# Causal mask by matmul, clamp split between VectorE and GpSimd, finer turns and a new order in a four-lane Flamingo block

## What is computed

```python
# layer 2, cross attention
attn = jnp.einsum('bhqd,bhkd->bhqk', q, k) * scale
attn = jnp.clip(attn, -CLAMP, CLAMP)            # CLAMP = 10000
attn = jax.nn.softmax(attn, axis=-1)
...
# layer 2, inner transformer ("self")
mask = jnp.triu(jnp.ones((s, s), dtype=bool), 1)
a = jax.nn.softmax(jnp.where(mask, -1000000000.0, a), axis=-1)
...
# layer 0, "bit": act_quant, one scale for each row (token)
scale = 127.0 / jnp.clip(jnp.max(jnp.abs(x), axis=-1, keepdims=True), 1e-05)
return jnp.clip(jnp.round(x * scale), -128, 127) / scale
```

## Time and profile before

| | us |
|---|---|
| median of 3 runs | 2759.86 (2751.84 to 2760.4) |
| the profiled execution, its own time | 2746.58 |
| its span, first to last instruction | 2745.4 |
| PE / PEld busy | 2523.2 / 2047.6 |
| DVE busy | 2182.1 |
| ACT busy | 1674.9 |
| POOL busy | 1134.7 |

### The profile page before, as it was taken

How to read it: one execution, slowest core, us unless ns; L and a number is a source line. 1 busy time by engine, 2 the same in 40 slices (tenths; PEclk the granted TensorE clock), 3 DMA queues, 4 the chain that set the end, 5 groups by cost and what they waited for, 6 DMA issues and landing times.

```text
span 2745.4 us, 66343 instructions
## 1 busy us (share of the span) xinstructions
PE 2523.2 (92%) x26308; PEld 2047.6 (75%) x26308; DVE 2182.1 (79%) x4794; ACT 1674.9 (61%) x4539; POOL 1134.7 (41%) x1981
## 2 busy tenths in 40 slices
PE   6897989898899989899999999999998989999999
PEld 4676767777677767777777777777777878778777
DVE  7778687888788686887777777778878787778998
ACT  4565767666566666666566556556666565556544
POOL 2132323323443543434554544434243333335776
PEclk9898989999899999999999999999999999999999
DMA  6000000000011221000011221000000000000110
GB/s 193 3 21 15 17 9 19 17 13 23 11 48 45 72 68 49 26 13 29 15 53 50 78 82 44 28 25 16 15 26 22 17 17 23 22 5 21 32 39 26
DMA packets 84190, 92.49 MB, mean 34 GB/s; under 512 B 15333, under 2 KB 77289, under 8 KB 83881
## 3 DMA queue, kind: packets, MB, share of 16 engines
q1 hardware_dynamic: 75432, 59.91, 7.1%
q0 software_dynamic: 8448, 28.34, 3.6%
HBM read 65.36 MB, written 22.85 MB: 32 GB/s over the span
## 4 chain that ended last, share of the span: by engine, by line
PE 46%; DVE 35%; ACT 7%; POOL 6%; issue 4%; DMA 1%; SPq 0%; DVEq 0%; POOLq 0%
PE psum L353 11%; PE psum L346 8%; DVE tiny L745 6%; DVE big L753 5%; PE psum L377 5%; PE psum L412 5%; PE psum L386 3%; PE psum L547 2%; PE psum L370 2%; PE psum L427 2%; DVE big L832 2%; PE psum L360 2%; DVE big L836 2%; DVE xn L726 2%; PE psum L367 2%
## 5 line engine op out<-in xcount | busy, mean ns | idle before, releaser
L1240 ACT ACTIVATE big<-big 128x512 f32<-128x512 f32 x512 | 312.3, 629 | 177.6 <-DVE big L753 176.0
L745 DVE TENSOR_REDUCE tiny<-psum 128x8 f32<-128x1024 f32 x256 | 312.3, 1220 | 43.5 <-PE psum L412 38.4
L753 DVE TENSOR_TENSOR big<-psum,tiny 128x512 f32<-128x512 f32 x512 | 329.4, 685 | 8.8
L1401 POOL TENSOR_SCALAR tiny<-mv 128x1 f32<-128x1 f32 x224 | 55.2, 246 | 675.6 <-DVE mv L716 673.7
L412 PE MATMUL psum<-head_keys,small 64*128 64x256 f32 x2048 | 293.9, 407 | 21.1 <-ACT big L1202 6.8
L386 PE MATMUL psum<-ident,big 64*128 64x64 f32 x5120 | 254.9, 233 | 37.9 <-ACT big L1240 18.8
L386 PEld LDWEIGHTS psum<-ident,big 64*128 64x128 f32 x5120 | 211.4, 142 | 103.7 <-ACT big L1240 43.5
L1418 POOL TENSOR_TENSOR head_keys<-big,head_rows 128x512 f32<-128x512 f32 x256 | 266.3, 1049 | 0.4
L1202 ACT ACTIVATE big<-psum 128x512 f32<-128x512 f32 x384 | 212.8, 598 | 63.9 <-PE psum L386 59.6
L1443 POOL TENSOR_TENSOR big<-big,tiny 128x512 f32<-128x512 f32 x128 | 136.7, 1074 | 271.0 <-DVE tiny L788 270.3
L412 PEld LDWEIGHTS psum<-head_keys,small 64*128 64x128 f32 x2048 | 187.3, 192 | 71.0 <-issue 46.0
(11 more groups left out here) (336 smaller groups left out, 6633.3 us busy)
## 6 DMA issues: line engine op xcount, KB each, us to landing
ctxT<-in_ctxT SPq DMA_DIRECT2D x64, 128.0 KB, 2.2
after_L_xattn<-x SPq DMA_DIRECT2D x64, 128.0 KB, 1.7
mixture_out<-spare SPq DMA_DIRECT2D x46, 128.0 KB, 1.7
x_in<-in_x SPq DMA_DIRECT2D x32, 128.0 KB, 2.2
mixture_in<-xn SPq DMA_DIRECT2D x32, 128.0 KB, 1.7
x_in<-after_L_xattn SPq DMA_DIRECT2D x32, 128.0 KB, 2.1
w_bits<-after_L_xattn SPq DMA_DIRECT2D x32, 128.0 KB, 2.3
spare<-in_L_w SPq DMA_DIRECT2D x2, 1024.0 KB, 6.4
```

Of the source, the lines that this page charges most:

```text
L745: dve.tensor_reduce(top, s8, AX.X, ALU.max).then_inc(*t.dve.tell(p, f"{l}.top{r}"))
L753: dve.tensor_tensor(t.e[half], s8[:, mine, :], top[:, mine].rearrange("p (h o) -> p h o", o=1).to_broadcast([P, CH, S]), ALU.subtract).the ...
L1240: last = act.activation(flat, flat, ACT.Exp, scale=DH ** -0.5)
```

## The change

1. **Causal mask.** The DVE pass L742 is gone. Ahead of the scores of `self`, PE writes the mask into the banks with 4 bf16 matmuls of 256 columns (`causal_rows`), and the scores are accumulated on top. The two bf16 constants `sooner` and `masked` are made on POOL during setup.
2. **Clamp.** The DVE pass L738 is gone. The 8 maxima are clamped (128x8), the subtraction becomes a `scalar_tensor_tensor` that also holds the lower bound, and POOL then takes the minimum with 0 on each half (128x512, four times per lane and pass); the exponential waits for POOL.
3. **Row scales.** `diag` and `diag2` are gone; PE transposes the scale column, broadcast over 128 columns.
4. **Finer turns.** On DVE a turn now ends after nearly every instruction whose result the next one needs; on PE long groups of matmuls are split in two or three turns.
5. **Order.** All five strings of `ORDER` are new.

```diff
-def features_T(pe, bank, wt, src, outs):
-    for j, n in enumerate(outs):
+def features_T(pe, bank, wt, src, outs, j0=0):
+    for j, n in enumerate(outs, j0):
...
+def causal_rows(pe, m, t):
+
+    for k in range(2):
+        for half in range(2):
+            rows = slice(half * P // 2, (half + 1) * P // 2)
+            later = t.ab[:, half, :].rearrange("p (h s) -> p h s", s=S)[:, :, k * P // 2:(k + 1) * P // 2]
+            pe.matmul(later, m.sooner[rows, k, :],
+                      m.masked[rows, :].rearrange("p (o s) -> p o s", o=1).to_broadcast([P // 2, CH, P // 2]),
+                      start=k == 0, stop=False)
...
     for r in range(2):
-        pe.wait_ge(*t.pool.at(p, f"{l}.keys{r}"))
         if r == 0:
             pe.wait_ge(*t.act.at(p, f"{l}.v" if l == "self" else f"{l}.q"))
         else:
             pe.wait_ge(*t.act.at(p, f"{l}.eT1"))
+        if l == "self":
+            causal_rows(pe, m, t)
+            yield
+        pe.wait_ge(*t.pool.at(p, f"{l}.keys{r}"))
...
-    context_values(pe, t.b, t.a, t, m.kv[l], range(KD)).then_inc(*t.pe.tell(p, f"{l}.kv"))
+    context_values(pe, t.a, t, m.kv[l], range(KD))
+    yield
+    context_rest(pe, t.b, t.a, t, m.kv[l], range(KD)).then_inc(*t.pe.tell(p, f"{l}.kv"))
...
-    pe.wait_ge(*t.dve.at(p, f"{l}.diag"))
-    pe.matmul(t.b[:, 0:S], m.ones[:], t.diag, start=True, stop=True).then_inc(*t.pe.tell(p, f"{l}.rows"))
+    pe.wait_ge(*t.dve.at(p, f"{l}.sc"))
+    pe.transpose(t.b[:, 0:S], t.tiny[:, 4:5].to_broadcast([P, S]), m.ident[:]).then_inc(*t.pe.tell(p, f"{l}.rows"))
...
-    features_T(pe, t.a, m.w["up"], t.xnT, range(0, 4)).then_inc(*t.pe.tell(p, f"{l}.up0"))
+    features_T(pe, t.a, m.w["up"], t.xnT, range(0, 2))
+    yield
+    features_T(pe, t.a, m.w["up"], t.xnT, range(2, 4), 2).then_inc(*t.pe.tell(p, f"{l}.up0"))
...
     dve.bn_stats(t.stats[:], src).then_inc(*t.dve.tell(p, f"{l}.st{sub}"))
+    yield
     dve.wait_ge(*t.dve.at(p, f"{l}.st{sub}"))
...
         dve.wait_ge(*t.pe.at(p, f"{l}.s{r}"))
+        dve.tensor_reduce(top, s8, AX.X, ALU.max).then_inc(*t.dve.tell(p, f"{l}.top{r}"))
+        yield
+        dve.wait_ge(*t.dve.at(p, f"{l}.top{r}"))
         if l == "L2":
-            flat = t.ab.rearrange("p r s -> p (r s)")
-            dve.tensor_scalar(flat, flat, CLAMP / DH ** -0.5, -CLAMP / DH ** -0.5, ALU.min, ALU.max
+            dve.tensor_scalar(top, top, CLAMP / DH ** -0.5, -CLAMP / DH ** -0.5, ALU.min, ALU.max
                               ).then_inc(*t.dve.tell(p, f"{l}.clip{r}"))
+            yield
             dve.wait_ge(*t.dve.at(p, f"{l}.clip{r}"))
-        if l == "self":
-            dve.tensor_tensor(s8, s8, m.causal[:].rearrange("p (o s) -> p o s", o=1).to_broadcast([P, 2 * CH, S]),
-                              ALU.min).then_inc(*t.dve.tell(p, f"{l}.mask{r}"))
-            dve.wait_ge(*t.dve.at(p, f"{l}.mask{r}"))
-        dve.tensor_reduce(top, s8, AX.X, ALU.max).then_inc(*t.dve.tell(p, f"{l}.top{r}"))
-        dve.wait_ge(*t.dve.at(p, f"{l}.top{r}"))
...
         for half in range(2):
             mine = slice(CH * half, CH * (half + 1))
-            dve.tensor_tensor(t.e[half], s8[:, mine, :],
-                              top[:, mine].rearrange("p (h o) -> p h o", o=1).to_broadcast([P, CH, S]), ALU.subtract
-                              ).then_inc(*t.dve.tell(p, f"{l}.e{2 * r + half}"))
-        yield
+            shift = top[:, mine].rearrange("p (h o) -> p h o", o=1).to_broadcast([P, CH, S])
+            if l == "L2":
+                dve.scalar_tensor_tensor(t.e[half], s8[:, mine, :], -CLAMP / DH ** -0.5, shift, ALU.max, ALU.subtract
+                                         ).then_inc(*t.dve.tell(p, f"{l}.e{2 * r + half}"))
+            else:
+                dve.tensor_tensor(t.e[half], s8[:, mine, :], shift, ALU.subtract
+                                  ).then_inc(*t.dve.tell(p, f"{l}.e{2 * r + half}"))
+            yield
...
-    then(dve.scalar_tensor_tensor(wt, lg, 0.0, m.first_of[:], ALU.is_equal, ALU.mult), "hot")
+    yield from then(dve.scalar_tensor_tensor(wt, lg, 0.0, m.first_of[:], ALU.is_equal, ALU.mult), "hot")
...
-                act.wait_ge(*t.dve.at(p, f"{l}.e{c}"))
+                if l == "L2":
+                    act.wait_ge(*t.pool.at(p, f"{l}.below{c}"))
+                else:
+                    act.wait_ge(*t.dve.at(p, f"{l}.e{c}"))
...
+    if l == "L2":
+        for c in range(4):
+            e = t.e[c % 2].rearrange("p h s -> p (h s)")
+            pool.wait_ge(*t.dve.at(p, f"{l}.e{c}"))
+            pool.tensor_scalar(e, e, 0.0, None, ALU.min).then_inc(*t.pool.tell(p, f"{l}.below{c}"))
+            yield
```

More of the change, by code:

```diff
@@ L47 @@
 BIASED = ()
-SPREAD = {"L2": "clip", "self": "mask"}
+SPREAD = {"L2": "clip"}
 STAGE = {
@@ L83, in narrow_signals @@
     if l in SPREAD:
[L84 removed]
+        dve = dve.replace("top0", "top0 " + SPREAD[l] + "0").replace("top1", "top1 " + SPREAD[l] + "1")
     return dve
@@ L411, in pe_heads @@
                 rows = slice(half * P // 2, (half + 1) * P // 2)
-                last = pe.matmul(t.ab[:, half, cols], t.qT[rows, r, :], keys[rows, cols], start=True, stop=True)
+                last = pe.matmul(t.ab[:, half, cols], t.qT[rows, r, :], keys[rows, cols], start=l != "self",
+                                 stop=l != "self" or cols.start > 0)
         last.then_inc(*t.pe.tell(p, f"{l}.s{r}"))
@@ L833, in dve_bitlinear @@
                                             t.act_h[:, k, 1:S], ALU.mult, ALU.add)
-        then(last, f"left{half}")
+        yield from then(last, f"left{half}")
         for k in ks:
@@ L924, in dve_plan @@
-    then(dve.tensor_tensor(one, nt, room[:, E1 - 1:2 * E1 - 1], ALU.add), "e1")
-    then(dve.tensor_tensor(two, one, room[:, 3 * E1 - 2:4 * E1 - 2], ALU.add), "e2")
-    then(dve.tensor_tensor(ends, two, room[:, 5 * E1 - 4:6 * E1 - 4], ALU.add), "e4")
+    yield from then(dve.tensor_scalar(nt, ends, -MAGIC, None, ALU.add), "down")
+    yield from then(dve.tensor_tensor(one, nt, room[:, E1 - 1:2 * E1 - 1], ALU.add), "e1")
+    yield from then(dve.tensor_tensor(two, one, room[:, 3 * E1 - 2:4 * E1 - 2], ALU.add), "e2")
@@ L927, in dve_plan @@
+    yield from then(dve.tensor_tensor(ends, two, room[:, 5 * E1 - 4:6 * E1 - 4], ALU.add), "e4")
     yield
-    then(dve.tensor_tensor(base, ends, nt, ALU.subtract), "nt")
-    then(dve.tensor_scalar(base, base, float(P), None, ALU.mult), "base")
-    then(dve.tensor_tensor(own, rank, base.rearrange("p (o e) -> p o e", o=1).to_broadcast([P, MIX, E1]), ALU.add), "at")
+    yield from then(dve.tensor_tensor(base, ends, nt, ALU.subtract), "nt")
+    yield from then(dve.tensor_scalar(base, base, float(P), None, ALU.mult), "base")
@@ L1597, in pool_program @@
                                   pattern=[[-DH, CH]], channel_multiplier=1)
+    for half in range(2):
+        rows = slice(half * P // 2, (half + 1) * P // 2)
+        for k in range(2):
+            pool.affine_select(out=m.sooner[rows, k, :], in_=m.sooner[rows, k, :], compare_op=ALU.is_ge, fill=0.0,
+                               base=k * P // 2 - 1, pattern=[[-1, P]], channel_multiplier=1)
+        last = pool.affine_select(out=m.masked[rows, :], in_=m.masked[rows, :], compare_op=ALU.not_equal,
+                                  fill=4 * MASKED, base=0, pattern=[[-1, P // 2]], channel_multiplier=1)
     last.then_inc(*tell(0, "setup.band"))
```

340 lines of the change are left out of this document (193 added, 147 removed), and 4 rows, old and new, of the table STAGE.

## The result

The changed kernel takes 2690.87 us (2685.39 to 2695.82), the kernel before 2756.86 us on the same chip: a ratio of 0.9758, 95% interval 0.9736 to 0.9781. By that ratio it is 67 us less (66 by the two medians), where 61 were forecast. The profiled execution took 2694.11 us, with a span of 2692.9.

What follows compares the result with a forecast made beforehand. PE was the bound, held up mostly by DVE, directly or through ACT. First half -40 idle and -20 clock, second half -22, mask +21: -61 us, giving 2699 us; 2645 to 2751 inside this case, 2645 to 2770 for 8 in 10.

Steps and rivals of the forecast that it cites:

- the first half: 60 to 1320 us of the span: PE idle time to fall by 40 us, low-clock loss by 20 us.
- The second half: 1320 to 2500 us: 22 us less PE idle time, against 21 us more PE work for the mask.
- The minimum's price: POOL's 128x512 minimum in `L2`, 128 times: 1.07 us each, bounds 0.246 to 1.074, 137 us more POOL work.
- the sign against me: Among the signs that would show the prediction wrong: a mean of POOL's minimum over 1.5 us.
- the third rival: POOL becomes the late engine in the second half, by longer rounds and waiting norms: +45 us, 2805 us; chance 0.12.
- a third: Share taken of the second half's 65 us PE idle time, as DVE loses some 160 us but `L2` is later: -22 us.
- DVE's account: DVE's work over the whole kernel: -177.5 + 12.3 - 66 + 18 = -213 us, about 54 us in the first half.
- The pairs: Dependent neighbours on DVE: 598 fewer stand directly behind the row they wait for, 0.11 us each, 66 us less.
- The collision that I feared: DVE instructions with two SBUF tensors slowed under POOL's minima in the second half: 36 hits of about 0.5 us, 18 us.
- The mask on PE: 256 mask matmuls ahead of the scores of `self`: 21 us more PE work, bounds 14 and 37 us.
- DVE was in the way: Denied by a rival: PE's idle time comes from chain latencies and static order, time stays 2752 to 2768 us; chance 0.12.
- The full gain: Rival: PE idle time and clock loss fall further in both halves, mask costs 14: -126 us, 2634 us; chance 0.12.

Runs made afterwards that it cites:

- e3: The change with the minimum with 0 on DVE, straight behind each subtraction, instead of on POOL; ratio 0.9666 to the kernel before.
- e4: The change with no minimum with 0 anywhere, the upper bound only on the maxima; ratio 0.9553 to the kernel before.
- e6: The change with the mask pass back on DVE and no mask matmuls on PE; ratio 0.9944 to the kernel before.
- e7: The change with the mask matmuls on PE laid twice in each self round; ratio 0.9803 to the kernel before.
- e12: The change with the old clamp pass back on DVE and no minimum on POOL; ratio 0.9727 to the kernel before.
- e5: The change with every POOL minimum done twice in a row; ratio 1.0800 to the kernel before.
- e8: The change with its split chains of dependent DVE instructions rejoined in one turn each, order and operations unchanged; ratio 1.0125 to the kernel before.
- e2: The change's operations with the order strings and long turns of the kernel before, minimum on DVE; 2727.64 us, ratio 0.9946 to the kernel before.
- e11: The change with the scaled identities back on DVE and matmuls by ones in place of the transposes; ratio 0.9838 to the kernel before.
- e10: The change with only the norms' statistics and their aggregation rejoined in one DVE turn; ratio 0.9823 to the kernel before.

## Why the prediction held, and where its steps did not

**The size of the gain, and the first half: right.** 67 us came where 61 were forecast. In the profiled pair, 52 us apart, the first half gave 52 of a forecast 60. PE's idle time there fell by 29 us (forecast 40), its clock rose from 0.95 to 0.97 as forecast, and its busy time fell by 23, of which the clock can have no more than 12 (forecast 20), because 11 are transposes that I had costed at nothing.

**The second half: wrong.** Forecast were -22 us of idle time and +21 for the mask; measured were +18 of idle time and -12 of busy time. That the sums, -1 and +6 us, lie close is luck. Three steps of the working failed, and they cancel in part:

- *The minimum's price.* I took 1.07 us with 0.246 to 1.074 as bounds, from the product of the same shape. It took 1.50, outside the bounds and at the mark that I had named as the sign against me. The chain to the second exponential is 1.22 + 0.24 + 0.69 + 1.50 + 1.50 + 0.63 = 5.8 us, not 4.88; on DVE (e3) it is 1.22 + 0.24 + 2 x (0.69 + 0.52) + 0.63 = 4.5. The step was to take a two-input operation as the upper bound of a one-input one: nothing in the trace excluded more. The Trainium skill ("GPSIMD Engine Reference", Engine selection), by which one-input work runs at roughly line rate and from which the estimate was 0.53 us, is further off: here one input took 1.4 times as long as two.
- *The mechanism of the third rival* was there in its first part, the 64 rounds whose chain is longer, and hardly in its second, the norms. POOL's minimum sets the time by the exponential that waits for it on ACT (91.2 us): DVE's wait for POOL's roots only went from 66.0 to 80.1 us, and that for the roots of `self` from 41.4 to 53.1. I had priced the longer chain of `L2` at 0.5 us a round and then let it vanish in "a third". The minimum costs 57 us (e4).
- *DVE's worth in the second half.* The mask pass was worth 51 to 63 of its 78 us (e6, e7), the clamp pass 48 of 78 (e12, e4).

**DVE's account: near in sum, by luck.** Forecast -213, measured -214.2; yet the sign that I had named, DVE busy near 2030 us, left the pairs out and missed by 62 us. The passes and the clamp of the maxima: -177.5 + 15.1, as forecast. The pairs, forecast at -66, have -35 us of busy time, as more overlap; gaps of up to 0.06 us also fell, by 25 us, but a gap is idle time and can't stand in this sum. The remaining -17 us are shorter durations, where I had +18 for collisions. Against the same four lines before, L1024, L1045, L1052 and L1053 take 7 us more; L786 takes 6 us less, and in the first half the conv steps of the earlier trace rows 14 us less (L895 and L899, 153 us against 167).

The collision that I feared of the minimum did not happen. All of DVE's durations together are 5 us less without the minima (e4), and 8 us *less* with twice as many (e5). In the change's trace, L786 took 0.45 us in the 13 cases that start under a minimum, 0.41 in the 89 with POOL idle, and 1.02 in the 28 that start under one of POOL's two-input products of 128x512. The price of a hit, 3.61 against 1.05 us, was read under such products and did not carry over to the minimum. (The 1.05 is the part that stands in the chain; the timeline has the same four at 1.13 us.)

```profile
L786 DVE TENSOR_SCALAR xn<-x,mv,tiny 128x256 f32<-128x256 f32 x192 | 101.1, 528 | 76.1 <-POOL tiny L1473 75.2
```

**The finer turns** were costed by the gap alone. e8 says that undoing them on DVE in this `ORDER` costs 101 us, more than the whole gain; e2, with the old turns and the old order, says 77 us against e3, as much as the operations are worth in the new order (74). I had left turns and order 66 us of DVE work, and a share of that in the sum.

**The mask on PE:** forecast 21, its group 25.0, its cost by doubling 12 us (good to 9), and 9 net of what the scores lose. The lower bound of 14 us has no row behind it. **The transposes:** forecast nothing, measured 11 us less PE work. **The range:** idle terms doubled or halved, with the mask at 14 or 37 us, make 2630 to 2746 us and not the 2645 to 2751 of the prediction; 2690.87 lies in both.

**The rivals.** DVE was in the way: passes that return cost 22 us (22 us of DVE work and 12 of PE's, e11) and 51 us (78 us of DVE work, e6). The full gain was not there, but the change with no minimum (e4), which leaves out the clamp's upper bound on the scores, comes to 0.9553, near the 2634 us (0.954) of that rival.

**Open.** PE's busy time in the second half fell by 12 us though mask matmuls were added. By the measure above (19.1 us for the mask, 10.6 less for the scores), 8 us less are the remainders of the context (`context_rest`, whose turn was split from the rest) and 3 us are 8 matmuls on the other side of the cut; the last 10 us are spread over many groups. The split turns on PE and the five strings of `ORDER` were not tried one by one, so how the 77 us divide between turns and order is not shown. Why the new order with the old operations loses 26 us in the second half was not tried.

## What to carry over

Before an operation leaves a busy engine for a slower one in the same chain, compare the length of the chain to the next waiter, not the busy shares, and measure the one instruction first. Here the freed engine was worth 15 us in the old order and 74 in one made for it. And once PE waits, count the clock too: in e5, 190 us more in a chain came back as 287.

## What the runs showed of the hardware

- GpSimd's in-place minimum of 128x512 fp32 with a constant took 1.50 us (1.475 to 1.750), its two-input product of the same shape 1.06 us, the same minimum on VectorE 0.52 us (e3).
- VectorE instructions of L786 that started under that one-input minimum took 0.45 us, under a two-input GpSimd product of 128x512 1.02 us, and with GpSimd idle 0.41 us (the change).
- 148 us more idle time of PE in a half (e5) went with a granted clock of 0.91 instead of 0.99, which means 2.4 GHz granted for less of the time, and 114 us more busy time for the same matmuls.
- Dependent neighbours on VectorE cost 0.10 us more of its time than independent ones, in e8 and e10 alike.
- An fp32 transpose of a broadcast column leaves half the records of the fp32 matmul in its place: 0.31 against 0.50 us for one scale row.
